# The preparation of a decoder kernel: x is loaded a second time, features on the partitions, and normalised there; no turns of x on TensorE

## The chip, the cores and the metric

The kernel runs on one core of a Trainium2 chip, as one program in one launch. The metric is device time in microseconds (us); lower is better. Instructions run on TensorE (PE in the profile), VectorE (DVE), ScalarE (ACT) and GpSimd (POOL); all transfers are issued by SyncE (SP).

## The reference

A decoder layer over x of 16 sequences x 128 tokens x 1024 features, in float32:

```python
x = x + latent_attention(layernorm(x), w_q_down, w_q_up_nope, w_q_up_rope, w_kv_down, w_k_rope, w_uk, w_uv, w_out)
x = x + cross(layernorm(x), ctx)      # a softmax attention on ctx
x = x + ffn(layernorm(x), k0, k1, k2) # three layers with weights of +-1
# layernorm(x) = (x - mean) / sqrt(var + 1e-5), over the 1024 features of a token
# the start of the attention, which is what the change touches (h = layernorm(x)):
c_q, c_kv, k_rope = h @ w_q_down, h @ w_kv_down, h @ w_k_rope    # 384, 128 and 64 columns
```

## The kernel before

Four stages follow each other: the preparation, the attention proper (quads of heads), the cross attention and the feed-forward. Float32 products are made of three passes over numbers cut into a high part (`fp32r`, a copy by ACT) and a low part (the difference, by DVE or POOL): high x high, high x low, low x high (`three_passes`, L53 to L55).

Only the preparation is changed. It projects the normalised x onto 640 columns (five groups of 128: three of queries, one of keys and values, one of rope keys). x comes in four chunks of 512 tokens (i = 0 to 3), each with eight tiles of 128 features (k = 0 to 7). One (i, k) is called **step** s = 8i + k here, and Ts is the time at which PE starts step s. A step is 15 matmuls of 512 columns: three passes for each of the five groups. Its moving operand is the normalised tile with features on the partitions, `hT_hi` and `hT_lo`, in three slots (`SLICES`).

How a tile gets there before: DVE takes mean and variance of each of the chunk's four sequences (`moments`, two BN_STATS and one BN_AGGR), ACT the root (`root`), DVE the inverse, and DVE (for chunk 0 ACT) normalises it in place, tokens on the partitions. In step s PE turns tile s + 2 by four transposes into the PSUM bank `prep_turned` (`turn_x`, L660), ACT copies the high part out of the bank (L1028), and DVE takes the low part (L1471). While chunk i is projected, DVE does the moments of chunk i + 1 in steps k = 0 to 3 and normalises in k = 1 to 4.

All engines run a program written out by hand, in order; an engine that waits for a semaphore waits with everything behind it. Beside the projections stand, by `BESIDE`: absorbed weights of the first heads (A after steps 4 and 6, B after 12 and 14), the first rope query (`rope`, 18 matmuls, after step 26) and two latent queries (after 28 and 30). At k = 7 of a chunk ACT and DVE take the five results out of PSUM (`query`, `keys`, `rope_keys`). Of a chunk's rope keys DVE makes two products; POOL adds them (`rope_key_sum`, L1301); ACT copies the sum twice at k = 0 of the next chunk (`rope_keys`, L1045, L1046), and POOL makes its low part (`rope_keys_low`, L1306). At k = 2 PE turns the values back (`turn_kv`). In step 24 ACT cuts the raw rope weights (L1128) and POOL makes their low part (`cut_rope`, L1320), for which PE waits before the rope query of step 26 (`wqr_lo`). The weights of the projection are cut once at the start, ACT the high and POOL the low parts (`cut_w_down`, L1296).

Of the kernel before, what the change touches and what calls it, by code (L numbers as in the profile page):

```python
# [15 lines left out]
P = 128  # L16
# [41 lines left out]
def decoder(nc, a, scratch, out_d):  # L58
# [13 lines left out]

    x, w_down, w_heads, w_rope, context, signs, consts = (
# [7 lines left out]
    PIECES = (slice(0, 1), slice(1, 2), slice(2, 4), slice(4, KT))  # L81
# [5 lines left out]
    turns = [("x", 0), ("x", 1)]  # L87
    for g in range(KT * N):
        if g + 2 < KT * N:
            turns.append(("x", g + 2))  # L90
        if g % KT == 2 and g > KT:
            turns.append(("kv", g // KT - 1))
    turns.append(("kv", N - 1))
    turn_at = {of: z for z, of in enumerate(turns)}

# [10 lines left out]
    with ctx:  # L106
# [47 lines left out]
        xt = [home(92160, "pj_x0", [P, BPC, D]), home(124928, "pj_x1", [P, BPC, D])]  # L154
# [9 lines left out]
        std, rstd, shift = (home(200832 + 32 * i, f"pj_{n}", [P, BPC]) for i, n in enumerate(("std", "rstd", "shift")))  # L164
# [38 lines left out]
        def sem(name):  # L203
# [17 lines left out]
        x_in = [[sem(f"pj_x_in{i}_{t}") for t in range(BPC)] for i in range(2)]  # L221
        w_in = [sem(f"pj_w_in{j}") for j in range(len(PIECES))]
        zeroed, eps_set = sem("pj_zeroed"), sem("pj_eps_set")
        var_ready, std_ready, rstd_done, shift_ready, first_hn_ready, hn_ready = (
            sem(f"pj_{n}") for n in ("var_ready", "std_ready", "rstd_done", "shift_ready", "first_hn_ready", "hn_ready"))
# [83 lines left out]
        x_chunks = x.rearrange("(c b p) d -> c p b d", c=CHUNKS, p=P)  # L309
        x1_chunks = x1_d.rearrange("(c b p) d -> c p b d", c=CPG, p=P)  # L310
# [52 lines left out]
        def _(sp):  # L363
# [50 lines left out]
            def load_x_tile(i, t):  # L414
                sp.dma_start(xt[i % 2][:, t, :], x_chunks[ORDER[i]][:, t, :]).then_inc(x_in[i % 2][t], 16)

            def load_w_down(j):
                rows = PIECES[j]
                sp.dma_start(w_raw[:, rows, :], w_down[:, rows, :]).then_inc(w_in[j], 16)

            def preparation():
                for t in range(BPC):
                    load_x_tile(0, t)
                load_w_down(0)
                sp.dma_start(ident[:], consts["ident"]).then_inc(ident_in, 16)
                load_w_down(1)
                load_w_down(2)
                load_w_down(3)
                for p in range(2):
# [3 lines left out]
                load_pair(0, 0, 0)  # L433
                load_pair(0, 1, 1)
                for t in range(BPC):
                    load_x_tile(1, t)
                for to, name in ((k_tab, "k_tab"), (mask, "mask"), (cos, "cos"), (sin, "sin")):
                    sp.dma_start(to[:], consts[name]).then_inc(const_in, 16)
# [5 lines left out]
                def store_keys(i):  # L444
                    sp.wait_ge(zeroed, 1)
                    sp.wait_ge(kr_lo, i + 1)
                    sp.wait_ge(prep_turn_taken, turn_at["kv", i] + 1)
                    sp.dma_start(tok_d[i][:, KT_HI:PACK], as_f32(tok[:, i, KT_HI:PACK])).then_inc(key_out[i], 16)

                def x_free(i):  # L450
                    sp.wait_ge(prep_turn_ready, turn_at["x", KT * i + KT - 1] + 1)

                sp.wait_ge(ab_mm, 2)
                load_head(0, 0, 0)
                x_free(0)
                for t in range(BPC):
                    load_x_tile(2, t)
                store_wabs(0, 0, 2)
                sp.wait_ge(ab_mm, 4)
                load_head(0, 1, 1)  # L460
                store_wabs(0, 1, 4)
                store_queries(0)
                store_keys(0)
                sp.wait_ge(ab_mm, 6)
                load_head(0, 2, 0)
                x_free(1)
                for t in range(BPC):
                    load_x_tile(3, t)
                sp.wait_ge(ab_mm, 8)
                load_head(0, 3, 1)  # L470
                store_wvo(0, 0, 8)
                store_queries(1)
                store_keys(1)

                x_free(2)
                load_raw_rope(0)
                store_wqr(0)
                relayout(0, 0)
                x_free(3)
# [1389 lines left out]
```

## Time and profile before

| | before |
|---|---|
| median of 3 runs | 2090.48 us (2086.85 to 2091.75) |
| the profiled execution: its time | 2087.33 us |
| its span, first to last instruction | 2085.1 us |
| PE busy | 2059.7 us, 99% |
| DVE, ACT, POOL busy | 61%, 37%, 22% |
| granted TensorE clock, mean | 0.999 |
| the first matmul of the projections | 16.68 us |
| the first matmul of step 24 follows a turn that starts at | 121.14 us |

How to read it: a matmul's row lasts longer than the distance to the next one, since they are pipelined; so steps are measured from start to start. The same holds for DVE, ACT and POOL, where an instruction that follows directly starts up to 0.1 us before the row of the one ahead ends.

### The profile page before, as it was taken

To read this page: it belongs to the slowest core of one execution; us is meant where nothing else is said; L and a number is where in the kernel's file an instruction comes from. 1 tells how busy PE (TensorE), PEld (TensorE's weight loads), DVE (VectorE), ACT (ScalarE), POOL (GpSimd) and SP (SyncE) were. 2 spreads that over 40 slices of the span, in tenths; PEclk is the share of its full clock that TensorE was granted. 3 is DMA by queue.
4 is the path that set the end of the run, shared out by engine and by line. 5 is a ranking of instruction groups with operands and counts; after the bars stand their busy time and mean duration, and the time that the engine had idled before them with its cause. 6 is when DMAs were issued, how large, how long until landed. Compare 5 with 4: busy or idle time off the path is not lost.

```text
span 2085.1 us, 30084 instructions
## 1 busy us (share of the span) xinstructions
PE 2059.7 (99%) x10746; PEld 1742.2 (84%) x10746; DVE 1271.5 (61%) x2114; ACT 775.6 (37%) x2018; POOL 450.8 (22%) x406
## 2 busy tenths in 40 slices
PE   6999999999999999999999999999999999999999
PEld 5787888888888888888888888888888778888887
DVE  4636666667666676666666666666667772433321
ACT  4324444444444353433333333333333455232221
POOL 2013333333324242321111212112121212000000
PEclk9999999999999999999999999999999999999999
DMA  5516353535353453666534244342435281102011
GB/s 223 237 59 224 106 175 107 197 114 206 122 185 121 158 170 109 225 212 227 155 108 141 73 144 136 106 156 70 151 116 202 101 315 69 54 28 81 1 41 41
DMA packets 63593, 284.78 MB, mean 137 GB/s; under 512 B 6704, under 2 KB 7344, under 8 KB 52016
## 3 DMA queue, kind: packets, MB, share of 16 engines
q1 hardware_dynamic: 63536, 284.00, 39.5%
q8 instruction: 38, 0.62, 0.1%
q14 instruction: 19, 0.16, 0.0%
HBM read 172.83 MB, written 111.15 MB: 136 GB/s over the span
## 4 chain that ended last, share of the span: by engine, by line
PE 97%; DVE 1%; DMA 1%; ACT 1%; issue 0%; POOL 0%; DVEq 0%; SPq 0%; POOLq 0%; ACTq 0%
PE at_out L53 12%; PE at_out L54 11%; PE at_out L55 11%; PE at_qbank L55 7%; PE at_qbank L53 7%; PE at_qbank L54 7%; PE at_qbank L967 6%; PE at_qbank L968 6%; PE at_score L756 4%; PE at_score L754 3%; PE at_turned L763 3%; PE at_value L55 2%; PE at_value L54 2%; PE at_value L53 2%; PE at_score L755 1%; PE at_value L984 1%
## 5 line engine op out<-in xcount | busy, mean ns | idle before, releaser
L1573 DVE TENSOR_TENSOR at_acc<-at_out,at_acc 128x512 f32<-128x512 f32 x512 | 352.2, 688 | 116.7 <-PE at_out L55 109.9
L53 PE MATMUL at_out<-at_wvo,at_val_hi 128*128 128x512 f32 x1024 | 403.2, 394 | 2.4 <-DVE at_acc L1573 2.4
L54 PE MATMUL at_out<-at_wvo,at_val_hi 128*128 128x512 f32 x1024 | 401.4, 392 | 0.0
L55 PE MATMUL at_out<-at_wvo,at_val_lo 128*128 128x512 f32 x1024 | 400.1, 391 | 0.0
L1087 ACT ACTIVATE at_probs<-at_probs,at_row_stats 128x128 f32<-128x128 f32 x512 | 199.8, 391 | 357.3 <-DVE at_row_stats L1551 357.3
L1325 POOL TENSOR_TENSOR at_probs<-at_probs,at_row_stats 128x512 f32<-128x512 f32 x128 | 133.4, 1042 | 582.7 <-DVE at_row_stats L1556 582.7
L55 PEld LDWEIGHTS at_out<-at_wvo,at_val_lo 128*128 128x128 f32 x1024 | 192.6, 188 | 43.0
L53 PEld LDWEIGHTS at_out<-at_wvo,at_val_hi 128*128 128x128 f32 x1024 | 193.3, 189 | 37.5 <-DVE at_acc L1573 3.5
L54 PEld LDWEIGHTS at_out<-at_wvo,at_val_hi 128*128 128x128 f32 x1024 | 193.2, 189 | 32.4
L1093 ACT ACTIVATE at_pT_hi<-at_turned 128x512 fp32r<-128x512 f32 x128 | 76.5, 597 | 319.4 <-PE at_turned L763 319.4
L756 PE MATMUL at_score<-at_tok,at_qrope 128*128 128x256 f32 x512 | 170.4, 333 | 0.0
L754 PE MATMUL at_score<-at_tok,at_qlat 128*128 128x256 f32 x512 | 154.5, 302 | 0.0
L53 PE MATMUL at_qbank<-at_tok,at_wabs 128*128 128x512 f32 x384 | 149.6, 390 | 0.0
L55 PE MATMUL at_qbank<-at_tok,at_wabs 128*128 128x512 f32 x384 | 149.4, 389 | 0.0
L54 PE MATMUL at_qbank<-at_tok,at_wabs 128*128 128x512 f32 x384 | 149.4, 389 | 0.0
L1524 DVE TENSOR_TENSOR at_qlat<-at_qbank,at_qlat 128x512 fp32r<-128x512 f32 x128 | 88.5, 691 | 99.7 <-ACT at_qlat L1073 99.0
L1332 POOL TENSOR_TENSOR at_rope_tmp<-at_rope_tmp 128x512 f32<-128x512 f32 x64 | 81.5, 1296 | 201.3 <-DVE at_rope_tmp L1529 201.2
L1073 ACT ACTIVATE at_qlat<-at_qbank 128x512 fp32r<-128x512 f32 x128 | 76.6, 599 | 124.5 <-PE at_qbank L55 124.5
L755 PE MATMUL at_score<-at_tok,at_qlat 128*128 128x128 f32 x512 | 113.7, 222 | 0.0
L1556 DVE RECIPROCAL at_row_stats<-at_row_stats 128x4 f32<-128x4 f32 x128 | 22.8, 178 | 142.8 <-ACT at_probs L1087 142.8
L1560 DVE TENSOR_TENSOR at_pT_lo<-at_turned,at_pT_hi 128x512 fp32r<-128x512 f32 x128 | 87.9, 687 | 27.0 <-ACT at_pT_hi L1093 27.0
L1316 POOL TENSOR_TENSOR ab_low<-ab_raw,ab_proj_hi 128x512 fp32r<-128x512 f32 x58 | 75.3, 1298 | 129.6 <-ACT ab_proj_hi L1069 129.6
(193 smaller groups left out, 4356.2 us busy)
## 6 DMA issues: line engine op xcount, KB each, us to landing
wvo_d<-at_wvo SPq DMA_DIRECT2D x16, 2048.0 KB, 8.6
parts_d<-at_rope_parts SPq DMA_DIRECT2D x32, 1024.0 KB, 7.0
at_qrope<-parts_d SPq DMA_DIRECT2D x128, 256.0 KB, 5.0
at_wvo<-wvo_d SPq DMA_DIRECT2D x16, 2048.0 KB, 8.4
ab_raw<-in_w_heads SPq DMA_DIRECT2D x32, 576.0 KB, 4.6
cr_ctx<-in_context SPq DMA_DIRECT2D x16, 1024.0 KB, 6.9
wabs_d<-at_wabs SPq DMA_DIRECT2D x16, 768.0 KB, 7.6
at_wabs<-wabs_d SPq DMA_DIRECT2D x16, 768.0 KB, 5.3
```

The costliest lines, as they stand in the source:

```text
L53: pe.matmul(out, w_hi, x_hi, start=first, stop=False)
L54: pe.matmul(out, w_hi, x_lo, start=False, stop=False)
L55: return pe.matmul(out, w_lo, x_hi, start=False, stop=last)
L754: pe.matmul(score[:, j], q_hi, keys[:, :, cols], start=True, stop=False)
L755: pe.matmul(score[:, j, 0], q_lo, keys[:, 0, cols], start=False, stop=False)
L756: ins = pe.matmul(score[:, j], qrope[c][:, pair * PAIR + h, cols], rope_keys[:, :, cols], start=False, stop=True)
L967: pe.matmul(ff_lin[m % 2][:], wk, act_hi[of][k // 4][:, k % 4, :], start=k == 0, stop=False)
L968: ins = pe.matmul(ff_lin[m % 2][:], wk, act_lo[of][k // 4][:, k % 4, :], start=False, stop=k == KT - 1)
L1087: ins = act.activation(probs[i][:, j, :], probs[i][:, j, :], ACT.Exp, bias=nmax[i][:, j:j + 1], accum_out=sums[i][:, j:j + 1])
L1325: pool.tensor_tensor(probs[i][:], probs[i][:], rsum[i].unsqueeze(2).to_broadcast([P, PARTS, SEQ]), ALU.mult).then_inc(probs_ready, 1)
L1524: dve.tensor_tensor(qlat[u % 2][:, 1, h, :], qbank[use % 2][:], as_f32(qlat[u % 2][:, 0, h, :]), ALU.subtract).then_inc(q_taken, 1)
L1573: dve.tensor_tensor(at, outb[n][:], at, ALU.add).then_inc(added, 1)
```

## The change

x is given to the kernel a second time, laid out with features on the partitions (`x_turned`, made on the host). The copy with tokens on the partitions (`xn`) now serves for the moments alone. Mean and inverse deviation of a token must lie along the free dimension then, the same on every partition: PE makes this by four transposes each of a column that is broadcast (`spread`), into a bank, and ACT copies it to `means` and `rdevs` (128x512 each, two buffers). A tile then goes this way: DVE subtracts the means (`centre_x`), POOL multiplies by the inverse deviations (`scale_x`), ACT copies the high part (`cut_x`, now from SBUF), DVE takes the low part (`cut_x`, both operands now in SBUF). Tile 0 is scaled by DVE instead. The spreads of chunk i + 1 stand in step k = 5 of chunk i. Slots of `hT` are now released by PE's step (`tile_used`). The weights are cut in five pieces and not four. Each of `xn` and `xt` has one buffer; SP's loads go in smaller parts between the others.

```diff
@@ SyncE: xt is loaded by two tiles
+            def load_turned(i, j):
+                if i:
+                    sp.wait_ge(prep_turn_taken, lo_at["x", KT * (i - 1) + 2 * j + 1] + 1)
+                tiles = slice(2 * j, 2 * j + 2)
+                sp.dma_start(xt[:, tiles, :], x_turned[ORDER[i]][:, tiles, :]).then_inc(xt_in[j], 16)
@@ TensorE
-                for t in range(BPC):
-                    ins = pe.transpose(prep_turned[:, t * P:(t + 1) * P], xt[i % 2][:, t, k * P:(k + 1) * P], ident[:])
+            def spread(to, i, t, of):
+                return pe.transpose(to[:, t * P:(t + 1) * P], of.to_broadcast([P, P]), ident[:])
+            def spread_rdevs(i):
+                pe.wait_ge(rstd_done, BPC * (i + 1))
+                pe.wait_ge(prep_turn_hi, hi_at["m", i] + 1)
+                for t in range(BPC):
+                    ins = spread(prep_turned, i, t, rstd[:, t:t + 1])
+                ins.then_inc(prep_turn_ready, 1)
@@ TensorE, preparation()
-                        s = KT * i + k
-                        if s and s + 2 < KT * N:
-                            turn_x(s + 2)
                         for m in range(5):
                             project(i, m, k)
-                            if s == 0 and m in (0, 2):
-                                turn_x(m // 2 + 1)
+                            if k == 5 and i + 1 < N:
+                                if m == 0:
+                                    spread_means(i + 1)
+                                elif m == 3:
+                                    spread_rdevs(i + 1)
@@ ScalarE
+            def cut_x(s):
+                act.wait_ge(hn_ready, s + 1)
+                if s >= SLICES:
...
+                        act.wait_ge(tile_used, (KT - 1) * i + k + 1)
+                act.activation(hT_hi[:, s % SLICES, :], xt[:, s % KT, :], ACT.Copy).then_inc(prep_turn_hi, 1)
@@ ScalarE, preparation()
                         s = KT * i + k + 2
                         if s < KT * N:
-                            turn_x(s)
+                            cut_x(s)
+                        if (i, k) == (0, 1):
+                            cut_w_down(3)
+                            cut_w_down(4)
                         if k == 0 and i:
                             rope_keys(i - 1)
                         if k == 2 and i:
                             kv_values(i - 1)
+                        if k == 5 and i + 1 < N:
+                            take_spread("m", i + 1)
+                            take_spread("r", i + 1)
                         if k < BPC and i < N - 1:
                             root(i + 1, k)
@@ GpSimd
+            def scale_x(s):
...
+                pool.wait_ge(centred, s + 1)
+                of = xt[:, s % KT, :]
+                pool.tensor_tensor(of, of, rdevs[s // KT % 2][:], ALU.mult).then_inc(hn_ready, 1)
             def opening():
-                for i in range(N - 1):
-                    rope_key_sum(i)
-                    rope_keys_low(i)
-                cut_rope(0)
+                cut_w_down(0)
+                for s in range(1, KT * N):
+                    scale_x(s)
+                    if s < len(PIECES):
+                        cut_w_down(s)
+                    if s >= KT and s % KT == 3:
+                        rope_key_sum(s // KT - 1)
+                    if s >= KT and s % KT == 4:
+                        rope_keys_low(s // KT - 1)
+                    if s == KT * (N - 1) + 5:
+                        cut_rope(0)
@@ VectorE, preparation(), s = KT * i + k
-                        if s < KT * N:
-                            turn_x(s)
+                        if s + 2 < KT * N:
+                            cut_x(s + 2)
+                        if s + 3 < KT * N:
+                            centre_x(s + 3)
                         if i < N - 1:
                             if k < BPC:
                                 moments(i + 1, k)
                             if 1 <= k <= BPC:
-                                normalise(i + 1, k - 1)
+                                inverse(i + 1, k - 1)
```

On GpSimd, the end of the preparation before: `pj_k_rot` is the sum of a chunk's rope keys, `at_tok` its low part, `at_wqr` the low part of the rope weights, `at_rope_tmp` the first rope query.

```order
L1301 TENSOR_TENSOR pj_k_rot<-pj_k_rot,pj_k_sin 64x512
L1306 TENSOR_TENSOR at_tok<-pj_k_rot,at_tok 64x512
L1320 TENSOR_TENSOR at_wqr<-at_rope_tmp,at_wqr 128x768
L1332 TENSOR_TENSOR at_rope_tmp<-at_rope_tmp 128x512 x2
L1339 TENSOR_TENSOR at_rope_parts<-at_rope_tmp,at_rope_parts 128x512 x2
```

The same place with the change, from the scaling of tiles 24 to 27 (the first row) on.

```order
L1427 TENSOR_TENSOR pj_xt<-pj_xt,pj_rdevs_89 128x512 x4
L1380 TENSOR_TENSOR pj_k_rot<-pj_k_rot,pj_k_sin 64x512
L1427 TENSOR_TENSOR pj_xt<-pj_xt,pj_rdevs_89 128x512
L1385 TENSOR_TENSOR at_tok<-pj_k_rot,at_tok 64x512
L1427 TENSOR_TENSOR pj_xt<-pj_xt,pj_rdevs_89 128x512
L1399 TENSOR_TENSOR at_wqr<-at_rope_tmp,at_wqr 128x768
L1427 TENSOR_TENSOR pj_xt<-pj_xt,pj_rdevs_89 128x512 x2
L1411 TENSOR_TENSOR at_rope_tmp<-at_rope_tmp 128x512 x2
```

The sum now stands behind the scaling of tile 27, its low part behind that of tile 28, and the low part of the rope weights behind that of tile 29.

On ScalarE, steps 5 and 6 with the change (`at_wabs` are the two heads of absorption A): the copy of the means of the next chunk stands behind the cut of tile 7, the first row.

```order
L1104 ACTIVATE pj_hT_hi<-pj_xt 128x512
L1092 ACTIVATE pj_means_87<-at_out 128x512
L1092 ACTIVATE pj_rdevs_89<-at_out 128x512
L1104 ACTIVATE pj_hT_hi<-pj_xt 128x512
L1131 ACTIVATE at_wabs_58<-at_qbank 128x384 x2
```

Before, nothing but cuts stood there; now PE, between the fourth and the fifth group of step 5, waits for the second of these rows before it spreads the deviations.

## Rows read from the trace of the kernel before

**Rows 1.** The head of the page: span and busy time.

```profile
span 2085.1 us, 30084 instructions
...
PE 2059.7 (99%) x10746; PEld 1742.2 (84%) x10746; DVE 1271.5 (61%) x2114; ACT 775.6 (37%) x2018; POOL 450.8 (22%) x406
```

**Rows 2.** Who waited for whom on PE, whole span: us in total, times, longest.

```profile
PE at_out L660 <- ACT pj_x L1023: 14.2, 1, 14.2
```

**Rows 3.** Timeline of PE: start, duration, line, operands.

```profile
16.68 0.79 PE L53 MATMUL at_score<-pj_hT_hi,pj_w_hi 128*128 128x512 f32 x1 [1.41 <-DVE pj_hT_lo L1471]
...
24.18 0.63 PE L660 MATMUL at_out<-at_ident,pj_x 128*128 128x128 f32 x4
...
57.99 0.60 PE L660 MATMUL at_out<-at_ident,pj_x 128*128 128x128 f32 x4
61.88 0.60 PE L660 MATMUL at_out<-at_ident,pj_x 128*128 128x128 f32 x4
...
66.52 0.63 PE L660 MATMUL at_out<-at_ident,pj_x 128*128 128x128 f32 x4
...
121.14 0.60 PE L660 MATMUL at_out<-at_ident,pj_x 128*128 128x128 f32 x4
...
133.29 0.39 PE L53 MATMUL at_qbank<-at_tok,at_wqr 128*128 128x512 f32 x1
...
151.13 0.39 PE L53 MATMUL at_score<-pj_hT_hi,pj_w_hi 128*128 128x512 f32 x1
...
154.53 0.39 PE L53 MATMUL at_qbank<-at_tok,at_wabs 128*128 128x512 f32 x1
...
162.72 0.28 PE L754 MATMUL at_score<-at_tok,at_qlat 128*128 128x256 f32 x1
```

**Rows 4.** Timeline of DVE, of ScalarE and of GpSimd, columns as in rows 3.

```profile
23.34 0.69 DVE L1471 TENSOR_TENSOR pj_hT_lo<-at_out,pj_hT_hi 128x512 fp32r<-128x512 f32 x1 [2.80 <-ACT pj_hT_hi L1028]
23.95 1.27 DVE L1441 BATCH_NORM_STATS2 pj_stats<-pj_x 128x6 f32<-128x512 f32 x2
...
25.54 0.30 ACT L1019 ACTIVATE pj_std<-pj_mv,at_limits 128x1 f32<-128x1 f32 x1 [2.31 <-DVE pj_mv L1445]
25.74 0.58 ACT L1028 ACTIVATE pj_hT_hi<-at_out 128x512 fp32r<-128x512 f32 x1
...
125.16 0.63 ACT L1045 ACTIVATE at_tok<-pj_k_rot 64x512 fp32r<-64x512 f32 x1 [2.78 <-POOL pj_k_rot L1301]
...
126.46 0.85 ACT L1128 ACTIVATE at_wqr<-at_rope_tmp 128x768 fp32r<-128x768 f32 x1
...
123.84 1.28 POOL L1301 TENSOR_TENSOR pj_k_rot<-pj_k_rot,pj_k_sin 64x512 f32<-64x512 f32 x1 [27.89 <-DVE pj_k_sin L1492]
...
127.77 1.83 POOL L1320 TENSOR_TENSOR at_wqr<-at_rope_tmp,at_wqr 128x768 fp32r<-128x768 f32 x1
```

**Rows 5.** Groups of GpSimd's instructions, shapes apart: busy us, mean ns, idle before.

```profile
L1332 POOL TENSOR_TENSOR at_rope_tmp<-at_rope_tmp 128x512 f32<-128x512 f32 x64 | 81.5, 1296 | 201.3 <-DVE at_rope_tmp L1529 201.2
...
L1296 POOL TENSOR_TENSOR pj_w_lo<-pj_w_raw,pj_w_hi 128x1280 fp32r<-128x1280 f32 x1 | 2.9, 2921 | 0.9 <-ACT pj_w_hi L1015 0.9
```

**Rows 6.** Two lines: ns shortest, median, longest; L1759's window: us, DVE busy, count.

```profile
L1759 DVE TENSOR_TENSOR ff_odd<-ff_hid,ff_odd x32: 691/692/1272, 1728.0 to 2054.2; 128x512 fp32r<-128x512 f32 x32
...
L1419 POOL TENSOR_SCALAR ff_w<-ff_bits,ff_sign_mul,ff_sign_add x8: 1195/1203/1742, 1724.0 to 1733.3; 128x1024 fp32r<-128x1024 uint8 x8
...
1726.00:1734.00 8.00, 1.97 (x2) 1.00 0.00 2
```

**Rows 7.** PE around a wait: timeline, then a window (PE busy, clock, DMA).

```profile
197.00 0.80 PE L53 MATMUL at_out<-at_wvo,at_val_hi 128*128 128x512 f32 x1 [1.66 <-DVE at_acc L1573]
...
201.31 0.39 PE L53 MATMUL at_qbank<-at_tok,at_wqr 128*128 128x512 f32 x1
...
198.00:200.00 2.00, 2.00 (x6) 0.50 0.71 297
```

**Rows 8.** Window of the first 17 us, all engines; the last two columns are DMA share, GB/s.

```profile
0.00:17.00 17.00, 1.41 (x5) 1.04 (x6) 7.54 (x22) 10.13 (x14) 4.25 (x8) 1.00 0.92 356
```

More of the change, by code:

```diff
@@ L85, in decoder @@
     ROPE_AT = {1: 0, 4: 1}
-    turns = [("x", 0), ("x", 1)]
+    turns, highs = [("m", 0), ("r", 0)], [("m", 0), ("x", 0), ("r", 0), ("x", 1)]
     for g in range(KT * N):
         if g + 2 < KT * N:
-            turns.append(("x", g + 2))
+            highs.append(("x", g + 2))
         if g % KT == 2 and g > KT:
             turns.append(("kv", g // KT - 1))
+            highs.append(("kv", g // KT - 1))
+        if g % KT == 5 and g < KT * (N - 1):
+            turns += [("m", g // KT + 1), ("r", g // KT + 1)]
+            highs += [("m", g // KT + 1), ("r", g // KT + 1)]
     turns.append(("kv", N - 1))
+    highs.append(("kv", N - 1))
     turn_at = {of: z for z, of in enumerate(turns)}
+    hi_at = {of: z for z, of in enumerate(highs)}
+    lo_at = {of: z for z, of in enumerate(of for of in highs if of[0] in ("x", "kv"))}
     BESIDE = {(0, 4): ("A", 0), (0, 6): ("A", 1), (1, 4): ("B", 0), (1, 6): ("B", 1),
@@ L153, in decoder @@
         w_raw = home(67584, "pj_w_raw", [P, KT, WC])
-        xt = [home(92160, "pj_x0", [P, BPC, D]), home(124928, "pj_x1", [P, BPC, D])]
+        xn, xt = home(92160, "pj_xn", [P, BPC, D]), home(124928, "pj_xt", [P, KT, CH])
+        means = [home(o, f"pj_means{i}", [P, CH]) for i, o in enumerate((88064, 83968))]
+        rdevs = [home(o, f"pj_rdevs{i}", [P, CH]) for i, o in enumerate((90112, 86016))]
         w_hi = home(141312, "pj_w_hi", [P, KT, WC], F32R)
@@ L428, in preparation @@
                 load_w_down(3)
+                load_x_tile(1, 0)
+                load_turned(0, 2)
+                load_x_tile(1, 1)
+                load_x_tile(1, 2)
+                load_pair(0, 0, 0)
+                load_turned(0, 3)
+                load_x_tile(1, 3)
+                load_pair(0, 1, 1)
+                for to, name in ((k_tab, "k_tab"), (mask, "mask"), (cos, "cos"), (sin, "sin")):
+                    sp.dma_start(to[:], consts[name]).then_inc(const_in, 16)
                 for p in range(2):
@@ L461, in preparation @@
                 store_wabs(0, 1, 4)
+                load_turned(2, 0)
                 store_queries(0)
+                load_x_tile(3, 0)
+                load_turned(2, 1)
+                load_x_tile(3, 1)
                 store_keys(0)
+                load_x_tile(3, 2)
+                load_turned(2, 2)
+                load_x_tile(3, 3)
                 sp.wait_ge(ab_mm, 6)
                 load_head(0, 2, 0)
-                x_free(1)
-                for t in range(BPC):
-                    load_x_tile(3, t)
+                load_turned(2, 3)
                 sp.wait_ge(ab_mm, 8)
@@ L1100, in preparation @@
                 act.wait_ge(eps_set, 1)
[L1101 to L1102 removed]
+                act.activation(unused[:, 0:1], eps[:], ACT.Sqrt)
                 for t in range(BPC):
[L1104 to L1108 removed]
+                    root(0, t)
+                take_spread("m", 0)
+                cut_w_down(0)
+                cut_x(0)
+                take_spread("r", 0)
                 cut_w_down(1)
[L1110 removed]
+                cut_x(1)
                 cut_w_down(2)
[L1112 to L1113 removed]
                 first = USES_PREPARED
@@ L1377, in _ @@
             pool.wait_ge(zeroed, 1)
-            for j in range(len(PIECES)):
-                cut_w_down(j)
             def cross_root(b):
```

183 lines of the change are left out of this document (106 added, 77 removed).

## The prediction

> **What bounds the kernel now.** I read the page first. PE is busy 2059.7 of the span's 2085.1 us [rows 1], so in nearly every stretch PE's own instructions set the time, and the page's chain says the same. Next, the waits on PE: the only long one is the 14.2 us at the start, until ACT has normalised x [rows 2]. The preparation therefore runs at PE's pace, from the first projection at 16.68 to the first scores at 162.72 [rows 3]. Less work on PE there is worth its full time, but only as long as DVE, ACT and POOL stay ahead.
>
> Next, PE's timeline, for the price of a step. With a turn a step takes 61.88 - 57.99 = 3.89 us; without one (step 30) 154.53 - 151.13 = 3.40; with the turn of the values as well 66.52 - 61.88 = 4.63 [rows 3]. So four transposes cost 0.49, the turn of the values 0.74, and a step's 15 matmuls 3.40. Last, the other engines' timelines, for durations and for how soon one starts after another.
>
> **The change part by part: what PE saves.** 29 turns stand in steps 1 to 29: 29 x 0.49 = 14.2 us. The turns of tiles 1 and 2 stand in step 0, at the low clock: 16.68 to 24.18 is 7.5 us [rows 3]; 15 matmuls alone, started at the low clock, I put at 6.0: 1.5 saved. Added are six groups of four transposes in steps 5, 13 and 21: 6 x 0.49 = 2.9 lost. The start: ACT's four normalisations go; a copy of the means, two passes of DVE, the cut and the low part take their place. Counted through, the first projection starts at 15.6, 1.0 earlier (14.9 to 17.0, by who gets ahead of whom). Net: 14.2 + 1.5 - 2.9 + 1.0 = 13.8 us.
>
> **What the tile's way costs.** Before, a tile needed ACT and DVE after PE. Now the loop is: DVE low part, 0.61 until its next instruction starts [rows 4]; centring of the next tile, 0.69 (median of a DVE pass with two SBUF operands [rows 6]) + 0.08 until POOL starts; scaling 1.30 [rows 5] + 0.04 until ACT starts; ACT's cut 0.61 with hand-over [rows 4]. The sum is 3.33, against 3.40 of PE: even, with nothing to catch up with. In k = 0 to 3 DVE's moments are the longer way: 0.61 + 0.61 + 1.59 (23.95 to the root at 25.54) + 0.20 (root to cut) + 0.61 = 3.62 [rows 4]: each such step loses 0.2. Any other delay stays until PE has waited for it.
>
> **Delay at a chunk's start.** DVE takes the five results after its two passes of step k = 7 and is done 3.4 us after T(8i) (before: the sum, which follows its last product, starts at 123.84, 2.7 after the turn at 121.14 [rows 3, 4]; plus a pass of 0.6). Then, in order: low part 0.6, centring 0.8, POOL scaling 1.3, POOL's sum of the rope keys 1.3, which now stands behind that scaling; ACT's two copies of it 1.3, for which ACT waits with its cuts behind; for chunk 3 the cut of the rope weights 0.8 [rows 4]. Only then is tile 8i + 3 cut, at T(8i) + 9.3 (10.1 in chunk 3).
>
> **Wait 1, the rope weights, step 26.** On from T24 + 10.1: low part 0.6, centring 0.8, scaling of 28 1.3, POOL's low part of the keys 1.3 (DVE's pass stands still meanwhile), low part 0.6, centring 0.8, scaling of 29 1.3, low part of the rope weights 1.85 [rows 4, 5]: T24 + 18.6. PE is there after three steps and a turn of values: 3 x 3.40 + 0.74 = T24 + 10.9. It waits 7.6 us; before, the weights were cut at 129.6 and the rope query began at 133.29, right after its step [rows 3, 4]. Queued behind it are all steps from 27 on. Even with no delay before T26, the way from the free slot of tile 28 to these weights is 0.6 + 0.6 + 0.8 + 1.3 + 1.85 = 5.2 against 4.1 of PE: this wait can't vanish.
>
> **Wait 2, the spreads, steps 5, 13, 21.** PE needs the copy of the means before it spreads the deviations, after the fourth group. ACT makes it behind the cut of tile 8i + 7. In chunk 1: T8 + 9.3, four rounds of about 3.6 to 3.8 with the keys' and the values' work, then centring, scaling, cut and copy: T8 + 24.6. PE is there at T8 + 22.5, so it waits 2.2. In chunk 2 no absorbed weights slow PE down, and the moments of tile row 3 come 1.4 late as well: 1.4 + 2.2 = 3.6. In chunk 0 likewise 2.7.
>
> **Wait 3, step 4.** Here the question is whether DVE and POOL hinder each other. While POOL ran eight instructions without a gap, two of DVE's low parts with two SBUF operands fell among them: one took 1272 ns and not 692, the other did not (1.97 us for both), and one of POOL's took 1742 and not 1203 [rows 6]. I read this as one engine standing still for the other's instruction, when they meet. At the start POOL has low parts of 2.92 us [rows 5] for the weights between the scalings. If DVE's passes stand still behind them, tile 2's low part waits for one and tile 4's for another: tile 4 is ready at 36.0, when PE, after four steps, is free at 31.9: 4.0 us. If they don't, it is ready before PE: nothing.
> The Trainium skill (page SBUF — State Buffer, section Who interferes with whom) states that a DVE instruction with two SBUF inputs and a GpSimd instruction that reads SBUF exclude each other for an instruction's whole length. The trace agrees in one case of two. By the rule the sum holds the 4.0, by the undisturbed case it doesn't.
>
> **The sum.** Waits 4.0 + 2.7 + 2.2 + 3.6 + 7.6 = 20.1, against 13.8 gained: +6.3 us. PE's clock comes on top: after a wait of 1.66 us, twelve matmuls from 197.00 to 201.31 took 4.3 us and not 12 x 0.23 = 2.8, at a granted clock of 0.50, the level of 1.2 GHz [rows 7]: 1.5 us lost. The waits in steps 13, 21 and 26 can each bring that (what it costs in chunk 0 is taken up by the next wait there): 0 to 4.6, and I take 3.0, since the shortest of them need not drop it. +9.3 us on the profiled execution's 2087.33 gives 2096.6. The median of the runs stands 3.15 above that execution, so 2099.8, +0.45%. The attention behind is not touched: the first rope query is in memory some 168 us after the start, the scores ask for it at 169, so nothing is added there, but only a microsecond is to spare.
> SP issues 8.4 MB more. The queue moved 356 GB/s in the first 17 us [rows 8]; tiles 6 and 7 are behind 9.1 MB, so in by 26 us, and centred from 39 on: hidden.
>
> **The rivals.** (a) Faster: the lead holds. The two tiles of lead (6.8 us) could swallow the start of a chunk if DVE took its five results nearly at once (by T(8i) + 2 and not 3.4) and the passes were shorter than I count. Then only the 1.1 of wait 1 and under 2 of the rest remain: 13.8 - 3 = 11 us less, 2079. For it: PE's margin in steps 9 to 12 is only just used up in my count. Against it: POOL's order. It decides at wait 1: below 5 us the sum turns negative, if wait 3 isn't there.
> (b) DVE and POOL don't hinder each other: wait 3 goes, 0.6 in each of waits 1 and 2, up to 6 in all; with 3 for the clock 2094, at the border of what can be told.
> (c) The clock falls in every wait, and stays low through more of the following step, 2 to 3 us each, and the store and reload of the rope query come late for the scores: +16, 2106.
> (d) The second x comes late: it would need under 230 GB/s. Part of (c).
>
> **How the numbers follow.** Forecast 0.45, (a) 0.18, (b) 0.24, (c) with (d) 0.13. 0.2%, 4.2 us, is about what can be told from no change. (b) lies at that border: half of it is slower, half the same. Slower 0.45 + 0.13 + 0.12 = 0.70, same 0.12, faster 0.18. The range leaves out most of (a) and half of (c): 2084 to 2107; the forecast's own is 2095 to 2104.
>
> **What would show it.** Steps without a wait last 3.40 from start to start. Waits on PE: at the rope query of step 26 for POOL's low part of the rope weights, 5 to 9 us; at the spread of the deviations for ACT, about 2 us, three times; at step 4 for the low part of tile 4, 4 us, with DVE passes of up to 3 us beside POOL's cuts of the weights. ACT's copies of the rope keys wait 5 us and more. The granted clock falls behind these. Wrong it would be if DVE ran ahead of PE through the chunk's start, or if POOL's scaling took much less than 1.3 us.

## The result, and the profile after

The changed kernel takes 2097.93 us (median of 6 runs, 2095.93 to 2100.10), the kernel before 2089.18 beside it (6 runs, 2086.85 to 2091.75): ratio 1.0047, 95% interval 1.0036 to 1.0057. The profiled execution took 2098.8 us against 2087.33. The forecast was 2099.8, slower.

The head of the page, columns as in [rows 1]:

```profile
span 2097.0 us, 29990 instructions
...
PE 2055.1 (98%) x10650; PEld 1733.9 (83%) x10650; DVE 1287.8 (61%) x2131; ACT 774.7 (37%) x2023; POOL 491.9 (23%) x438
```

PE has 96 instructions and 4.6 us of work less, and the span is 11.9 us longer: PE now waits. For whom, in the first 200 us (us in total, times, longest; the kernel before has one wait of 14.2 in the preparation, at its start [rows 2]):

```profile
PE at_out L692 <- DMA at_ident<-in_ident: 9.3, 1, 9.3
PE at_score L53 <- DVE pj_hT_lo L1566: 8.0, 2, 4.4
PE at_qbank L53 <- POOL at_wqr L1399: 6.5, 1, 6.5
PE at_out L692 <- ACT pj_means L1092: 4.5, 3, 2.1
PE at_out L692 <- DVE pj_mv L1538: 1.3, 2, 1.1
...
PE at_score L817 <- DMA at_qrope<-parts_d: 0.7, 1, 0.7
PE at_score L53 <- DVE at_tok L1572: 0.5, 1, 0.5
```

The first of these, and 3.6 of the 8.0, lie ahead of the first projection.

PE's timeline, for the places of these waits:

```profile
15.61 0.80 PE L53 MATMUL at_score<-pj_hT_hi,pj_w_hi 128*128 128x512 f32 x1 [3.62 <-DVE pj_hT_lo L1566]
...
20.50 0.39 PE L53 MATMUL at_score<-pj_hT_hi,pj_w_hi 128*128 128x512 f32 x1
...
35.62 0.79 PE L53 MATMUL at_score<-pj_hT_hi,pj_w_hi 128*128 128x512 f32 x1 [4.39 <-DVE pj_hT_lo L1566]
...
46.14 0.62 PE L692 MATMUL at_out<-at_ident,pj_rstd 128*128 128x128 f32 x4 [0.69 <-ACT pj_means L1092]
...
80.16 0.62 PE L692 MATMUL at_out<-at_ident,pj_rstd 128*128 128x128 f32 x4 [1.79 <-ACT pj_means L1092]
...
109.97 0.65 PE L692 MATMUL at_out<-at_ident,pj_mv 128*128 128x128 f32 x4 [1.12 <-DVE pj_mv L1538]
...
114.73 0.62 PE L692 MATMUL at_out<-at_ident,pj_rstd 128*128 128x128 f32 x4 [2.06 <-ACT pj_means L1092]
...
123.36 0.50 PE L53 MATMUL at_score<-pj_hT_hi,pj_w_hi 128*128 128x512 f32 x1 [0.47 <-DVE at_tok L1572]
...
141.22 0.80 PE L53 MATMUL at_qbank<-at_tok,at_wqr 128*128 128x512 f32 x1 [6.51 <-POOL at_wqr L1399]
...
147.12 0.39 PE L53 MATMUL at_score<-pj_hT_hi,pj_w_hi 128*128 128x512 f32 x1
...
171.82 0.36 PE L817 MATMUL at_score<-at_tok,at_qlat 128*128 128x256 f32 x1 [0.72 <-DMA at_qrope<-parts_d]
...
183.13 1.96 PE L765 MATMUL at_qbank<-ab_raw 128*128 128x512 f32 x4 [0.92 <-DVE at_rope_tmp L1624]
...
205.06 0.39 PE L53 MATMUL at_value<-at_pT_hi,at_tok 128*128 128x256 f32 x1 [1.88 <-DVE at_pT_lo L1655]
...
207.70 0.80 PE L53 MATMUL at_out<-at_wvo,at_val_hi 128*128 128x512 f32 x1 [1.66 <-DVE at_acc L1668]
```

Read against [rows 3], the first projection is 1.07 us early (15.61 for 16.68), step 1 starts 3.7 before the turn that began it (20.50 for 24.18), the rope query is 7.93 late (141.22 for 133.29) and the scores 9.1 late (171.82 for 162.72). The output that starts at 197.00 in [rows 7] starts at 207.70, 10.7 late. So in these two executions 9.1 of the span's 11.9 us are lost in the preparation, and 2.8 behind it. They lie further apart than the medians, which differ by 8.75: the profiled execution of the kernel before is among its short ones, that of the changed kernel among its long ones.

### The profile page after: what moved, and what is told of

Same layout as the page of the kernel before. It is cut to its first block, busy times and chain, and to the rows that moved or that the text cites. A ratio compares the mean times of both kernels' runs of the same rounds, so it can differ in the third digit from the quotient of the medians.

```text
span 2097.0 us, 29990 instructions
## 1 busy us (share of the span) xinstructions
PE 2055.1 (98%) x10650; PEld 1733.9 (83%) x10650; DVE 1287.8 (61%) x2131; ACT 774.7 (37%) x2023; POOL 491.9 (23%) x438
## 4 chain that ended last, share of the span: by engine, by line
PE 90%; DVE 4%; DMA 2%; POOL 2%; ACT 1%; issue 1%; DVEq 1%; SPq 0%; ACTq 0%; POOLq 0%
PE at_out L53 11%; PE at_out L54 11%; PE at_out L55 11%; PE at_qbank L53 7%; PE at_qbank L55 7%; PE at_qbank L54 7%; PE at_qbank L1033 6%; PE at_qbank L1034 6%; PE at_score L819 4%; PE at_score L817 3%; PE at_turned L826 3%; PE at_value L55 1%; PE at_value L54 1%; PE at_value L53 1%; PE at_score L818 1%; PE at_value L1050 1%
```

## The experiments

Line numbers in the rows are those of each kernel. An edit stands on top of the changed kernel where no other is named, and "less" or "earlier" is against the changed kernel too. Each kernel was compared with the kernel before on the same chip.

Two things set the size of what can be read here. Starts and spans come from one profiled execution of each kernel, and executions of the same kernel differ (those of version 6 have spans from 2081.3 to 2087.6); where the medians say something else, they are given too. And the first projection starts at 15.61 in the changed kernel's profile, at 14.98 to 15.63 in those of the versions, whose start is the same: the load of the identity matrix, for which PE waits first (9.3 us there, 8.3 to 9.3 in the others), landed at another time. Up to 0.6 us of an "earlier" is that.

**1. The rope weights first.** GpSimd makes the low part of the rope weights two scalings earlier, behind that of tile 27.

```diff
-                    if s == KT * (N - 1) + 5:
+                    if s == KT * (N - 1) + 3:
                         cut_rope(0)
```

> The changed kernel with one step moved on GpSimd: the low part of the rope weights stands right behind the sum of the rope keys, ahead of the scaling of tiles 28 and 29. Theory (the order on GpSimd makes the wait at step 26): the 6.5 us wait for these weights goes, and the matmuls behind it run at the high clock: the span falls by 6.5 to 9 us, to 2088 to 2090.5. Rival (the tiles themselves are late, and the wait only moves to step 27 or to the scores of the first quad): the span stays above 2094, with a new wait on PE between 134 and 172 us.

Measured: 2090.71 us, ratio 1.0015 (1.0006 to 1.0025); span 2088.0, 9.0 less than the changed kernel's. The wait for `at_wqr` is gone. The scores start at 164.29, 7.5 earlier, and there a wait that was 0.7 is 2.2:

```profile
PE at_out L692 <- ACT pj_means L1092: 4.7, 3, 2.0
PE at_score L817 <- DMA at_qrope<-parts_d: 2.2, 1, 2.2
```

So one place in GpSimd's order is worth most of the loss: 7.5 us up to the scores (0.6 of it the earlier start) and 9.0 of the 11.9 in the span, while the medians lie 7.2 apart. The wait for the reloaded rope query, which stands next on the way, took back 1.5 of what the removed wait and the clock behind it gave.

**2. The means first.** ScalarE copies the means ahead of the cut of tile 8i + 7 and not behind it.

```diff
+                        if k == 5 and i + 1 < N:
+                            take_spread("m", i + 1)
                         s = KT * i + k + 2
                         if s < KT * N:
                             cut_x(s)
...
                         if k == 5 and i + 1 < N:
-                            take_spread("m", i + 1)
                             take_spread("r", i + 1)
```

> The changed kernel with one copy moved on ScalarE: in step 5 of a chunk the copy of the means stands ahead of the cut of tile 8i + 7 instead of behind it. Theory: the three waits at the spread of the deviations (0.7, 1.8 and 2.1 us) go and nothing takes their place at once; the span falls by 3 to 5 us, to 2092 to 2094. Rival (tiles are late anyway, these waits only take up what a wait behind them would have cost): the waits turn up again at the next tile or as a longer wait for the rope weights, and the span stays within 1 us.

Measured: 2095.20 us, 1.0033 (1.0023 to 1.0044), span 2095.2. The three waits for the means, 4.5 us together, are gone (those for the moments stay, 1.5), and the span is only 1.8 shorter (the medians: 2.7), less than the 3 to 5 of the theory. The lead is spent at once where step 24 needs the banks of the results of chunk 2, with 2.21 us for DVE instead of 0.47, and at the rope weights, which still cost 5.3:

```profile
PE at_qbank L53 <- POOL at_wqr L1402: 5.3, 1, 5.3
PE at_score L53 <- DVE at_tok L1575: 2.4, 2, 2.2
```

A wait in the middle of the preparation is worth only what no later wait takes up.

**3. Eight pieces of weights.** GpSimd's low parts of the projection weights are made tile by tile (640 columns each, one behind each scaling) and not in two passes of 640 and three of 1280. ScalarE cuts piece k + 3 in step k.

```diff
-    PIECES = (slice(0, 1), slice(1, 2), slice(2, 4), slice(4, 6), slice(6, KT))
+    PIECES = tuple(slice(j, j + 1) for j in range(KT))
...
-                        if (i, k) == (0, 1):
-                            cut_w_down(3)
-                            cut_w_down(4)
+                        if i == 0 and k + 3 < KT:
+                            cut_w_down(k + 3)
```

> The changed kernel with the weights of the projection cut in eight pieces of one tile each and not five, so that no instruction of GpSimd beside the first tiles is longer than 1.5 us. Theory (VectorE's passes with two SBUF operands stand still behind the 2.9 us cuts, and the scalings behind them too): the wait of 4.4 us at step 4 falls to under 1, and the span by 3 to 5 us, to 2092 to 2094. Rival (GpSimd has too much to do in chunk 0, however it is divided; eight pieces are 12.3 us and not 11.8): the wait moves to another step, and the span changes by under 1.5 us.

Measured: 2095.07 us, 1.0034 (1.0020 to 1.0047), span 2093.3, 3.7 less (the medians: 2.9). The scores start only 1.65 earlier (170.17). The wait of 4.4 at step 4 is gone, and at step 5 one of 0.69 has become 3.29. ScalarE's copy of the means, which PE awaits there, starts at 42.18 and has waited 0.92 for GpSimd's last piece, since the means of chunk 1 lie over the raw weights. The rest is the cut of tile 7 ahead of it, which came late (40.63): beside the low passes GpSimd's scalings of tiles 5, 6 and 7 follow each other at 4.05 us (31.23, 35.28, 39.32), where a step of PE takes 3.40.

```profile
42.92 0.62 PE L692 MATMUL at_out<-at_ident,pj_rstd 128*128 128x128 f32 x4 [3.29 <-ACT pj_means L1092]
```

**4. All three.** The edits of 1, 2 and 3 together.

> The three edits together: rope weights first, means first, eight pieces. Theory: each wait has its own cause, so the gains add, and the 13.8 us that were worked out for the missing turns and the earlier start come through: 2097 - 8 - 4 - 4 = 2081, 2078 to 2084 with what remains of the waits; faster than the kernel before by about 0.2%. Rival (the loop over four engines has no spare time against 3.40 us a step, so the waits come back elsewhere): 2085 to 2091, no faster than before.

Measured: 2085.38 us, 0.9990 (0.9981 to 0.9999); span 2085.3, above the 2078 to 2084 of the theory. The scores start at 159.26, 3.5 us before those of the kernel before [rows 3], with 2.2 of wait for the stored rope query. Even so the span is that of the kernel before, 2085.1: in this execution the 3.5 us are given back behind the scores. Half of them are gone by the product that starts at 173.95 in the kernel before and at 172.15 here:

```profile
172.15 1.95 PE L767 MATMUL at_qbank<-ab_raw 128*128 128x512 f32 x4 [0.92 <-DVE at_rope_tmp L1626]
```

From the first scores to this product are 12.89 us here, and 11.31 in the changed kernel (171.82 to 183.13), whose scores waited 0.7 and not 2.2. The granted clock from the one to the other is 0.87 here and 1.00 there. It is so in every version: 12.87 to 12.89 where the scores waited 2.2 or 2.3 us (1, 4 and 6), 11.30 or 11.31 in all where they waited 0.7 to 0.9. The wait for the stored rope query thus costs its 2.2 us and 1.6 of clock. At the output that starts at 197.00 in [rows 7] and here at 195.81, 1.2 of the 3.5 are left.

**5. PE kept busy.** In the changed kernel 26 matmuls of 512 columns into a free bank stand ahead of the wait for the rope weights; their result isn't used.

```diff
+                                pe.wait_ge(q_taken, first)
+                                for _ in range(26):
+                                    pe.matmul(qbank[1][:], w_hi[:, 0, 0:P], w_hi[:, 1, 0:CH], start=True, stop=True)
```

> The changed kernel with 26 more matmuls of 512 columns on PE ahead of its wait for the rope weights in step 26; they write a bank that nobody reads, and fill some 5.9 us of the 6.5 us wait. Theory (the 18 matmuls of the rope query took 5.9 us and not 4.1 since the clock had fallen in the wait): with PE busy through the wait they take 4.1 us, and the first scores and the span come 1.5 to 2.5 us earlier although PE does more. Rival (the clock's share is nothing in the end, since the way of the rope query through memory is what comes last): the rope query is shorter, the scores and the span are not.

Measured, one run: 2094.84 us, span 2093.0. First the window of 141 to 148 us in the changed kernel, then in this one. The columns are the stretch's length, busy time of PE, its loads, DVE, ACT and POOL, then granted clock, DMA share and GB/s:

```profile
141.00:148.00 7.00, 6.78 (x22) 5.49 (x23) 1.97 (x4) 0.00 (x0) 0.17 (x1) 0.73 0.27 112
```

```profile
141.00:148.00 7.00, 6.41 (x28) 5.29 (x29) 3.24 (x6) 0.00 (x0) 0.54 (x1) 1.00 0.27 112
```

The wait for the weights ends 0.4 later (141.59 against 141.22), but the clock behind it is 1.00 and not 0.73, and 28 matmul records fit where 22 did. The scores start 1.15 earlier (170.67), a little less than the 1.5 to 2.5 of the theory. The idle 6.5 us thus cost 1.6 us of clock on top of themselves: the 18 matmuls of the rope query took 5.9 us (141.22 to 147.12) and here 4.26 (141.59 to 145.85); 18 x 0.23 is 4.1.

**6. Rope sums ahead.** Version 4, and GpSimd adds the first rope query's products ahead of the scaling of tile 30, to have it stored earlier.

```diff
                 for s in range(1, KT * N):
+                    if s == KT * N - 2:
+                        rope_sums(first + 2)
                     scale_x(s)
...
-                rope_sums(first + 2)
```

> The three edits together, and on GpSimd the two sums of the first rope query ahead of the scaling of tiles 30 and 31. Theory (what the three edits uncovered, a wait of 2.2 us of the first scores for the rope query's way through memory, is again the order on GpSimd): the store of the query's parts comes 2 to 2.5 us earlier, that wait goes, and the span falls from 2085.3 to 2082 to 2083.5. Rival (transfers set the time after that: x for the accumulators and the raw rope weights of the next quad): the scores come earlier, the span stays above 2084.5.

Measured: 2085.86 us, 0.9986 (0.9977 to 0.9995), span 2086.1. This theory fell: the wait for the stored query is still 2.3, since the store is issued at the same time as in version 4 (147.84 for 147.86). The low parts of the query (`at_rope_parts`), not its sums, end that chain, and they still stand behind the scaling of the last tile:

```profile
143.58 1.29 POOL L1429 TENSOR_TENSOR pj_xt<-pj_xt,pj_rdevs 128x512 f32<-128x512 f32 x1 [2.07 <-DVE pj_xt L1560]
144.83 2.99 POOL L1420 TENSOR_TENSOR at_rope_parts<-at_rope_tmp,at_rope_parts 128x512 fp32r<-128x512 f32 x2
```

**7. The keys' sum ahead.** Version 6, and GpSimd adds a chunk's rope keys ahead of the scaling of tile 8i + 3 and not behind it.

```diff
-                    if s >= KT and s % KT == 3:
+                    if s >= KT and s % KT == 2:
                         rope_key_sum(s // KT - 1)
```

> As the kernel before in this list, and the sum of a chunk's rope keys ahead of the scaling of tile 8i + 3 on GpSimd, so that ScalarE, which waits for it with its cuts behind, goes on about 2 us earlier in steps 8, 16 and 24. Theory: the lead at a chunk's start is what the later waits live on, so the waits of 1.1 us for the moments in step 21 and of 2.2 us for VectorE's results at step 24 go or shrink, and the span falls by another 2 to 4 us, to 2079 to 2081. Rival (these two waits come from VectorE's own order, moments and results behind two passes a step): they stay, and the span changes by under 1 us.

Measured: 2083.32 us, 0.9975 (0.9965 to 0.9986), span 2081.6: 4.5 less than version 6 in the profiled executions, from one instruction moved over one other, and 2.5 less in the medians (the profiled execution of version 6, at 2087.92, is one of its longer ones). ScalarE, which waits for that sum with all its cuts behind, waits 3.56 us in chunk 3 and not 5.63:

```profile
122.28 0.63 ACT L1123 ACTIVATE at_tok<-pj_k_rot 64x512 fp32r<-64x512 f32 x1 [3.56 <-POOL pj_k_rot L1382]
```

Of the two waits on PE that the theory names, the one of 1.1 for the moments in step 21 is gone, and the one at step 24 is still 2.25. The scores start only 0.8 earlier (158.57 for 159.36), but they wait 0.7 for the stored query and not 2.3, and the stretch behind them takes 11.30 us instead of 12.89. So much of the gain comes from a wait that is short enough to leave the clock alone.

**8. Three turns less in the kernel before.** Of each turn of x from tile 2 on, one transpose of four is left; the result is without three quarters of those tiles.

```diff
-                for t in range(BPC):
+                for t in range(1 if s > 1 else BPC):
                     ins = pe.transpose(prep_turned[:, t * P:(t + 1) * P], xt[i % 2][:, t, k * P:(k + 1) * P], ident[:])
```

> The kernel before the change, in which a turn of x from tile 2 on turns only the first of the four sequences, so that three of its four transposes are left out and the rest of the bank keeps what stood there (the output is not the reference's). 30 x 3 x 0.12 us are taken off PE and nothing else is changed. Theory (PE's time in the turns counts in full): the first scores come 10 to 11.5 us earlier, and the span is 2074 to 2076. Rival (transfers or VectorE take a part of it back): the scores come early but the span is above 2078.

Measured: 2081.25 us, 0.9965 (0.9953 to 0.9977), span 2078.9, which is the rival's and not the 2074 to 2076 of the theory. The scores start at 155.78, 6.9 us earlier, where the matmuls left out are worth 10 to 11.5. The old way takes a third back too, most of it in 3.2 us of waits that the kernel before doesn't have:

```profile
PE at_out L660 <- DVE pj_hT_lo L1471: 2.0, 2, 1.7
...
PE at_out L667 <- DVE pj_hT_lo L1471: 1.2, 2, 0.6
```

**9. Own places for the means of chunk 1.** Version 7, with the means and deviations of chunk 1 where the rope weights come later, so that they wait for no low part.

```diff
-        means = [home(o, f"pj_means{i}", [P, CH]) for i, o in enumerate((88064, 83968))]
-        rdevs = [home(o, f"pj_rdevs{i}", [P, CH]) for i, o in enumerate((90112, 86016))]
+        means = [home(o, f"pj_means{i}", [P, CH]) for i, o in enumerate((88064, 61440, 88064, 83968))]
+        rdevs = [home(o, f"pj_rdevs{i}", [P, CH]) for i, o in enumerate((90112, 63488, 90112, 86016))]
...
-                if i == 1:
+                if i == 3:
                     act.wait_ge(w_lo_done, len(PIECES))
```

> The version with all five edits, and the spread means and deviations of chunk 1 in places of their own (free until step 24) instead of over the raw projection weights, so that ScalarE no longer waits for GpSimd's last low part of those weights before it takes them. Theory (TensorE's wait of 3.4 us at step 5 is that wait for the place alone): it falls under 0.8 us, step 24 starts some 2.5 to 3 us earlier, the scores start near 156 us, and the profiled span is 2.0 to 3.0 us below 2081.6. Rival (ScalarE is late with the means anyway, or step 6's tile is late next): the wait stays over 2 us or moves to steps 6 to 8, and the span stays within 1 us of 2081.6.

Measured: 2081.01 us, 0.9968 (0.9956 to 0.9981), span 2078.3, 3.3 less than version 7 (the medians: 2.3). The wait of 3.4 at step 5 is gone; of it 1.66 comes back at step 8, and the scores start 2.9 earlier than in version 7:

```profile
50.08 0.50 PE L53 MATMUL at_score<-pj_hT_hi,pj_w_hi 128*128 128x512 f32 x1 [1.66 <-DVE at_tok L1575]
...
114.46 0.61 PE L53 MATMUL at_score<-pj_hT_hi,pj_w_hi 128*128 128x512 f32 x1 [2.25 <-DVE at_tok L1575]
...
155.68 0.36 PE L819 MATMUL at_score<-at_tok,at_qlat 128*128 128x256 f32 x1 [0.71 <-DMA at_qrope<-parts_d]
```

This is the fastest kernel of the study that does the whole computation.

**10. Short low passes.** The changed kernel, where GpSimd's low passes over the weights of tiles 2 to 7 cover 64 of each tile's 640 columns. The low parts of the other columns are zero, so the result lacks them.

```diff
+                wide = slice(0, WC if j < 2 else 64)
-                pool.tensor_tensor(w_lo[:, rows, :], w_raw[:, rows, :], as_f32(w_hi[:, rows, :]),
+                pool.tensor_tensor(w_lo[:, rows, wide], w_raw[:, rows, wide], as_f32(w_hi[:, rows, wide]),
                                    ALU.subtract).then_inc(w_lo_done, 1)
...
+                pool.memset(as_f32(w_lo[:, 2:KT, 64:WC]), 0.0)
                 cut_w_down(0)
```

> The changed kernel, in which GpSimd's low passes over the projection weights for tiles 2 to 7 cover 64 of each tile's 640 columns (the rest is set to zero ahead of the first pass, so the low parts of those weights are left out of the result). Theory (DVE's own low passes of 2.76 and 2.69 us are long because they run beside GpSimd's, which take about 2.9 us there): with no long GpSimd pass beside them they fall to 0.69 to 1.3 us, TensorE's wait of 4.4 us at step 4 falls under 1 us, and step 5 starts 3.5 to 4.5 us earlier. Rival (the length comes from DVE's pass itself at that place, or from the load of x): the passes stay over 2.5 us and the wait at step 4 over 3 us.

Measured, one run: 2092.43 us, span 2090.6, 6.4 less. First DVE and GpSimd in the changed kernel, then DVE in this one:

```profile
21.06 2.76 DVE L1566 TENSOR_TENSOR pj_hT_lo<-pj_xt,pj_hT_hi 128x512 fp32r<-128x512 f32 x1 [1.85 <-ACT pj_hT_hi L1104]
...
32.87 2.69 DVE L1566 TENSOR_TENSOR pj_hT_lo<-pj_xt,pj_hT_hi 128x512 fp32r<-128x512 f32 x1 [3.26 <-ACT pj_hT_hi L1104]
...
20.32 2.95 POOL L1375 TENSOR_TENSOR pj_w_lo<-pj_w_raw,pj_w_hi 128x1280 fp32r<-128x1280 f32 x1
...
32.13 2.89 POOL L1375 TENSOR_TENSOR pj_w_lo<-pj_w_raw,pj_w_hi 128x1280 fp32r<-128x1280 f32 x1
```

```profile
20.80 0.69 DVE L1567 TENSOR_TENSOR pj_hT_lo<-pj_xt,pj_hT_hi 128x512 fp32r<-128x512 f32 x1 [1.84 <-ACT pj_hT_hi L1104]
...
28.12 0.69 DVE L1567 TENSOR_TENSOR pj_hT_lo<-pj_xt,pj_hT_hi 128x512 fp32r<-128x512 f32 x1 [0.83 <-ACT pj_hT_hi L1104]
```

The first row of DVE is the low part of tile 2, the second that of tile 4. The same DVE pass takes 2.76 us beside GpSimd's 2.95, and 0.69 without it; 21.06 + 2.76 = 23.82 and 20.32 + 2.95 = 23.27, so DVE's pass is done about one pass of its own (0.55) behind the end of GpSimd's. The wait at step 4 is gone, and the one at step 5 is down to 0.2. The scores start 6.0 earlier (165.84).

## Why the prediction was right

**What PE saves** was right in its parts. Steps without a wait last 3.40 (20.50 to 23.90). Step 0 took 4.89 and not the 6.0 that the sum has: its matmuls are back at 0.39 us after six at 0.63 to 0.80, so about 1.1 more was saved there. The start at 15.6 is 15.61.

**What the tile's way costs, and the delay at a chunk's start**, were right: ScalarE waits 5.61, 5.62 and 5.63 us for the sum of the rope keys in the three chunks ("5 us and more"). The order on GpSimd is the one counted:

```profile
129.05 1.28 POOL L1380 TENSOR_TENSOR pj_k_rot<-pj_k_rot,pj_k_sin 64x512 f32<-64x512 f32 x1
134.43 1.26 POOL L1427 TENSOR_TENSOR pj_xt<-pj_xt,pj_rdevs 128x512 f32<-128x512 f32 x1 [4.10 <-DVE pj_xt L1557]
135.65 1.26 POOL L1385 TENSOR_TENSOR at_tok<-pj_k_rot,at_tok 64x512 fp32r<-64x512 f32 x1
138.15 1.26 POOL L1427 TENSOR_TENSOR pj_xt<-pj_xt,pj_rdevs 128x512 f32<-128x512 f32 x1 [1.23 <-DVE pj_xt L1557]
139.37 1.80 POOL L1399 TENSOR_TENSOR at_wqr<-at_rope_tmp,at_wqr 128x768 fp32r<-128x768 f32 x1
```

**Wait 1** was put at 7.6 and is 6.51, with 0.47 ahead of step 24 for DVE's copies of the results, which the prediction didn't have. Counted from the start of step 24 (123.36), the rope weights are ready at 139.37 + 1.80, T24 + 17.8 where 18.6 was said. Experiment 1 shows its cause: GpSimd's order.

**Wait 2** was put at 2.7, 2.2 and 3.6, and is 0.69, 1.79, and 1.12 + 2.06 = 3.18: the last in two parts, of which the first (for the moments of the last row of tokens) had been named as late, but not as a wait of its own. The first was too large: the term took the waits as independent, but in chunk 0 the 4.39 at step 4 had given the other engines time to catch up. With step 4's wait gone, the one at step 5 is 3.29 in experiment 3, 0.92 of it for the last low part of the weights. In experiment 10, where the low passes are short, it is 0.2 without any wait at step 4: so what makes the tiles late there is GpSimd's work on the weights, and not the loop alone, as "likewise" had it. (The prediction's 2.2 for chunk 1 is 2.1 by its own 24.6 and 22.5, and its 3.4 for DVE's results is 3.3 by 2.7 and 0.6; nothing hangs on either.)

**Wait 3** was put at 4.0 and is 4.39. The question that [rows 6] left open, one disturbed pass of two, is answered by experiment 10. It matters which operands: at 12.93 a DVE pass that takes one operand from PSUM runs its 0.69 beside a low pass of GpSimd (12.87, 1.54), and the next, with both in SBUF, takes 1.42:

```profile
12.93 0.69 DVE L1562 TENSOR_TENSOR pj_xt<-pj_xt,at_qbank 128x512 f32<-128x512 f32 x1
13.54 1.42 DVE L1557 TENSOR_TENSOR pj_xt<-pj_xt,pj_means 128x512 f32<-128x512 f32 x1
```

Before the change, every low part of x took one operand from PSUM [rows 4]. The one at 23.34 there ran its 0.69 inside a low pass of GpSimd over four tiles' weights:

```profile
22.12 5.72 POOL L1296 TENSOR_TENSOR pj_w_lo<-pj_w_raw,pj_w_hi 128x2560 fp32r<-128x2560 f32 x1 [2.06 <-ACT pj_w_hi L1015]
```

The kernel's change of way is what brings DVE and GpSimd into each other's way. The Trainium skill (page SBUF — State Buffer, section Who interferes with whom) states as a rule that a DVE instruction with two inputs in SBUF and a GpSimd instruction that reads SBUF contend with each other, and the trace agrees, with 2.76 for 0.69 us.

**The sum.** The waits of 20.1 are 17.0 by the rows (4.39 + 0.69 + 1.79 + 3.18 + 0.47 + 6.51), and 0.72 more at the scores. **The clock** of 3.0 is 1.8 at the rope query and 1.7 at step 4, whose 15 matmuls took 5.12 us (35.62 to the absorbed heads) and not 3.40; the text had held the latter for taken up by the next wait. With 14.9 gained (13.8 and 1.1), 17.7 + 3.5 - 14.9 = 6.3 of the 9.1 are named. The other 2.8 lie in gaps that the view of waits doesn't list, as in step 16, where the first matmul of the fifth result starts 0.43 behind the one ahead of it and not 0.23, as DVE and ScalarE are just taking the results of chunk 1 out; they weren't followed one by one. Steps 16 and 24 last 3.82 and 3.89 us (89.90 to 93.72, 123.36 to 127.25) and not 3.40:

```profile
92.49 0.40 PE L55 MATMUL at_value<-pj_hT_hi,pj_w_lo 128*128 128x512 f32 x1
92.92 0.50 PE L53 MATMUL at_out<-pj_hT_hi,pj_w_hi 128*128 128x512 f32 x1
```

The preparation as a whole was to lose 9.3 and lost 9.1. That it comes so near is luck: the waits came out 2.4 smaller and step 0 1.1 better than in the sum, the clock 0.5 and the gaps 2.8 worse. What was right is the direction, the places of the three waits and the engine that it named at each.

**"The attention behind is not touched"** is the step that did not hold. The microsecond to spare at the scores was not there: they waited 0.72 for the rope query. That wait was short enough to cost nothing more, but in experiments 1, 4 and 6 the store, which stands behind GpSimd's last scaling, holds the scores up for 2.2 to 2.3 us. And 2.8 us were lost later. From the scores (+9.1) to the products at 183.13 (+9.2, 173.95 in the kernel before) the shift is the same; then the raw rope weights of the next heads, loaded at 194.89, are cut by ScalarE at 202.96, 8.07 later, where the kernel before has 6.79 (185.47 to 192.26):

```profile
192.26 0.85 ACT L1195 ACTIVATE at_wqr<-at_rope_tmp 128x768 fp32r<-128x768 f32 x1 [4.23 <-DMA at_rope_tmp<-in_w_rope]
```

```profile
202.96 0.84 ACT L1274 ACTIVATE at_wqr<-at_rope_tmp 128x768 fp32r<-128x768 f32 x1 [5.75 <-DMA at_rope_tmp<-in_w_rope]
```

ScalarE's next copy (`at_pT_hi`, 203.71) stands behind that cut, DVE's `at_pT_lo` (204.32) follows the copy, and PE waits for that 1.88 us (205.06) and not 0.36 (194.37): 1.5 of the 2.8. Another 1.0 comes at the low clock: between 207.70 and the next query at 212.99 are 5.3 us, where [rows 7] have 4.3. The last 0.2 or 0.3 weren't followed. Whether the change causes any of this isn't shown. That wait of 1.88 is 0.40 in experiment 5, 0.55 in 3, 1.38 in 10 and 1.55 in 2, whose edits all stand ahead of it, so it varies as much from one execution to the next. Why the load took 1.3 longer in this one isn't settled.

Behind the scores these 2.8 are the miss on the profiled execution, +11.5 us where +9.3 was forecast (0.2 less up to the scores, 0.4 less outside the span). In the medians the difference is 8.75, less than the preparation alone lost here. **The step from the execution to the median** added 3.15, from three runs; over six it is 1.85 for the kernel before, and for the changed kernel the median lies 0.87 below its profiled execution. So the forecast of the median had 2.2 too little up to the profiled execution and 4.0 too much from there on, and comes out 1.9 above the 2097.93 measured: two errors that offset each other, again by luck.

**Rivals.** (a) fell, as the order on GpSimd alone holds 7 us and more. (b) fell by experiment 10. (c) was partly true: the clock fell at two places of the preparation and not in all, and the rope query came 0.7 late for the scores. (d) did not occur: no wait of PE or DVE names a load of the second x behind the start.

## What to carry to other kernels

Before an engine's work goes to the others, write down their loop in order, instruction by instruction, and compare it with the time that is left of the first engine's step: here 3.33 us against 3.40, so that each late item stayed late until the first engine had waited for it. What is moved onto a strict-order queue is worth as much as its place in it: moving one low part by two places was worth 7 us in the medians, and one sum by one place 2.5. And a wait taken away shows the next one behind it, so that only versions with several edits beat the kernel before (0.9968 at best). Nor is a wait's length its whole price: at the scores 0.7 us cost 0.7, and 2.2 cost 3.8 with the clock. A difference of a few us between two single profiled executions is a weak measure of an edit; read it together with the medians and with landmarks ahead of and behind the edited place.

## What the runs showed of the hardware

The exclusion of DVE and GpSimd was measured more sharply than expected: a pass of DVE with both operands in SBUF took 2.76 us beside one of GpSimd of 2.95, and 0.69 without it; a pass with one operand in PSUM wasn't touched beside GpSimd's low passes (0.69 us at 12.93, and at 23.34 in the kernel before); nor were the moments of one tile row (1.28 us at 27.99, beside 2.97 of GpSimd that starts at the same time). GpSimd's pass gives way in turn: scalings of 1.28 us took 1.59 and 1.73 beside DVE's. After 6.5 us without work PE ran the 7 us from 141 to 148 at a mean granted clock of 0.73; with 26 matmuls in the gap at 1.00. After a wait of 2.2 us at the scores the stretch of 11.3 us behind it took 1.6 longer, in three of three profiles; after waits of 0.7 to 0.9 us it didn't, in eight of eight.
